# Causal mask carried by staircase rows in both score stacks, turn of the normalised rows placed between score units, keys of later batches written to DRAM in stack order

## The reference

```python
x = x + self_attn(layernorm(x), Wq, Wk, Wv, Wo)      # 16 heads of 8, rotary, causal
x = x + cross_attn(layernorm(x), ctx, W_kv, W_q, W_proj, b_proj)
x = x + moe(layernorm(x), gate_w, w1, b1, w2, b2)    # top 2 of 8, gelu, routed by the mean row
# inside self_attn:
attn = where(causal, -inf, q @ k.T / sqrt(8)); out = softmax(attn) @ v
```

## Time and profile before

| what | us |
|---|---|
| median of 3 runs | 183.94 (183.62 to 191.8) |
| the profiled execution | 183.63 |
| its span, first to last instruction | 181.8 |
| PE busy | 163.6 (90%) |
| DVE busy | 129.9 (71%) |
| ACT busy | 104.9 (58%) |
| POOL busy | 67.7 (37%) |

### The profile page before, as it was taken

How to read it: one execution, slowest core, us unless ns; L and a number is a source line. 1 busy time by engine, 2 the same in 40 slices (tenths; PEclk the granted TensorE clock), 3 DMA queues, 4 the chain that set the end, 5 groups by cost and what they waited for, 6 DMA issues and landing times.

```text
span 181.8 us, 4434 instructions
## 1 busy us (share of the span) xinstructions
PE 163.6 (90%) x1528; PEld 117.6 (65%) x1536; DVE 129.9 (71%) x500; ACT 104.9 (58%) x218; POOL 67.7 (37%) x132
## 2 busy tenths in 40 slices
PE   5778987979899799799999999999999998989994
PEld 4457765756666577467567556656666465879983
DVE  4488599597599879879988988999955463642110
ACT  2055531257566565665567766867746766972351
POOL 6836929178900660250232232201251071124220
PEclk9999998799999999999999999999999999999999
DMA  5914254157157245134035125104402501706400
GB/s 161 286 17 127 71 157 121 50 131 184 41 143 194 64 128 151 32 101 142 24 79 159 30 78 157 32 4 123 143 7 84 177 0 26 238 29 176 118 29 29
DMA packets 23329, 18.39 MB, mean 101 GB/s; under 512 B 2308, under 2 KB 21252, under 8 KB 22660
## 3 DMA queue, kind: packets, MB, share of 16 engines
q1 hardware_dynamic: 22552, 17.20, 34.0%
q10 hardware_dynamic: 756, 0.92, 1.8%
HBM read 12.08 MB, written 2.29 MB: 79 GB/s over the span
## 4 chain that ended last, share of the span: by engine, by line
PE 55%; DVE 23%; DMA 8%; issue 5%; SPq 3%; POOL 2%; ACT 2%; DVEq 0%; POOLq 0%; ACTq 0%
PE psV L975 11%; PE psA L929 9%; PE psB L953 8%; DVE negmax L663 8%; PE psA L1019 6%; DMA stackQ<-scratch 5%; PE psV L1036 4%; PE psM L843 4%; DMA ctx_tok<-ctx_dram 3%; DVE xn L616 3%; DVE masked L657 3%; PE psB L866 3%; PE psA L1036 2%; DVE stats L607 2%; PE psB L1019 2%
## 5 line engine op out<-in xcount | busy, mean ns | idle before, releaser
L797 ACT ACTIVATE E<-psB 128x512 f32<-128x512 f32 x112 | 62.1, 595 | 24.5 <-PE psB L958 10.2
L929 PE MATMUL psA<-stackK,stackQ 72*128 72x256 bf16 (+1 forms) x256 | 41.5, 260 | 5.1 <-DVE negmax L657 2.0
L663 DVE TENSOR_REDUCE negmax<-psA 128x2 f32<-128x512 f32 x64 | 40.6, 681 | 4.4 <-PE psA L929 4.2
L953 PE MATMUL psB<-stackQ,stackK 74*128 74x256 bf16 (+1 forms) x256 | 41.1, 259 | 0.4
L657 DVE CUSTOM_DVE_ANT_0 masked<-psA,row_mask 128x128 bf16<-128x128 f32 (+1 forms) x128 | 36.8, 347 | 6.0 <-PE psA L929 6.0
L929 PEld LDWEIGHTS psA<-stackK,stackQ 72*128 72x128 bf16 x256 | 21.7, 98 | 15.2 <-DVE negmax L663 3.0
L975 PE MATMUL psV<-E,V 128*18 128x256 f32 (+1 forms) x512 | 30.5, 356 | 0.0
L953 PEld LDWEIGHTS psB<-stackQ,stackK 74*128 74x128 bf16 x256 | 22.1, 97 | 6.7 <-ACT E L797 2.7
L513 POOL TENSOR_SCALAR rstd<-mv 128x2 f32<-128x2 f32 x12 | 2.7, 227 | 56.6 <-DVE mv L611 56.6
L975 PEld LDWEIGHTS psV<-E,V 128*18 128x18 f32 x512 | 11.9, 97 | 13.1 <-issue 6.6
L616 DVE TENSOR_SCALAR xn<-res,mv,rstd 128x128 f32<-128x128 f32 x24 | 10.0, 514 | 6.5 <-POOL rstd L514 6.4
(11 more groups left out here) (112 smaller groups left out, 249.5 us busy)
## 6 DMA issues: line engine op xcount, KB each, us to landing
stackK<-scratch SPq DMA_DIRECT2D x18, 192.0 KB
stackQ<-hid SPq DMA_DIRECT2D x36, 64.0 KB
w1s<-w_dram SPq DMA_DIRECT2D x8, 258.0 KB, 2.8
w2s<-w_dram SPq DMA_DIRECT2D x8, 256.0 KB, 4.2
stackQ<-scratch SPq DMA_DIRECT2D x2, 576.0 KB
stackK<-hid SPq DMA_DIRECT2D x16, 64.0 KB
scratch<-hid SPq DMA_DIRECT2D x4, 192.0 KB, 4.2
scratch<-parts_ctx SPq DMA_DIRECT2D x4, 192.0 KB, 6.6
```

Of the source, the lines that this page charges most:

```text
L663: dve.tensor_reduce(negmax[:, b, heads[0]:heads[-1] + 1:2, t], scores, AX_X, ALU.max, negate=True).then_inc(a_taken, 1)
L797: act.activation(dst, psB[:, bank].rearrange("p (h q) -> p h q", h=dst.shape[1]), ACT.Exp, scale=SCALE).then_inc(b_taken, 1)
L929: last = pe.matmul(psA[:, bank, i * keys:(i + 1) * keys], stackQ[0:ROWS, b, h, t * P:(t + 1) * P], stackK[0:ROWS, b, h, 0:keys], start=Tru ...
L953: last = pe.matmul(psB[:, bank, i * n:(i + 1) * n], stackK[:, b, h, t * P:(t + 1) * P], stackQ[:, b, h, q0:S], start=(s == 1 or i == 0), s ...
```

## The change

Four edits.

1. **Mask in the stacks.** The stacks get 48 more rows (`KEPT`; 120 in all, `CAUSAL`). Rows 72 to 119 hold a staircase of powers of two in keys (`kept_k`) and queries (`kept_q`) that makes the product over 120 rows of a diagonal 128x128 block hugely negative above the diagonal and leaves the rest alone. Rows 72, 73 are ones in `kept_k` and zeros in `kept_q`. POOL builds the two tiles (48 x 256) with 7 affine selects and 3 memsets in place of `mask16T` and `row_mask`. SP copies them, broadcast over 16 heads, to all batches (`stack_keep`): two DMAs of 768 KB for batches 0 and 1 together, two of 384 KB each for batch 2 and batch 3. A and B units of s=0 use 120 rows on the diagonal block and 72 or 74 elsewhere, so that products of 256 columns across a diagonal block become two of 128. The mask product L958 goes; job 0's A units, which run before the rows are there, get such a product instead. DVE takes maxima of s=0 with one reduction for a unit, as s=1 does. The two DMAs of ones go.
2. **`ln_turn`** of all jobs but the last moves from the end of one half to behind the first two units of the next.
3. **Keys in stack order.** `write_k` sends each part by its own DMA as soon as it is ready (3 of 64 KB instead of 1 of 192 KB) so that DRAM holds them in the order of the stack's rows; the source of each read is then [24 rows][8 KB].
4. New waits: PE's first A unit of a job and first B unit, and SP's first `max_rows`, wait for the kept rows (`kept_in`).

```diff
+KEPT = 48
+CAUSAL = ROWS + KEPT
-    start += [("stack_put", 0, 1), ("stack_fill", 0, 1)]
+    start += [("stack_put", 0, 1), ("stack_keep", 0, 0, 2), ("stack_fill", 0, 1), ("stack_keep", 0, 2, 1)]
+    put(14, "stack_keep", 0, 3, 1)
-        put(m + 4, "ln_turn", s + 1, b)
+        if (s, b) == (1, NB - 1):
+            put(m + 4, "ln_turn", s + 1, b)
+        else:
+            between.setdefault(m + 5, []).append(("ln_turn", s + 1, b))
-        order += [step for _, step in sorted(units, key=lambda unit: unit[0])]
+        units = [step for _, step in sorted(units, key=lambda unit: unit[0])]
+        order += units[:2] + between.get(half, []) + units[2:]
 # SP
+            def rows_k(s, b):
+                return scratch[s, b, 1].rearrange("i p t -> (i p t)").rearrange("(e t) -> e t", t=NH * S)
+            def write_k(s, b, src, ready):
+                rows = rows_k(s, b).rearrange("(d r) (h t) -> r d h t", r=NPART, h=NH)
+                for r in range(NPART):
+                    sp.wait_ge(ready, r + 1)
+                    sp.dma_start(rows[r], src[:, r]).then_inc((scr_k_self, scr_k)[s][b], 16)
             def read_k(s, b):
-                src = scratch[s, b, 1]
-                by_part = bass.AP(src.tensor, src.offset, [[NH * S, HD], [P * S, NPART], [1, NH * S]])
                 for i in range(NPART):
                     r = i * NPART * HD
-                    sp.dma_start(stackK[r:r + NPART * HD, b], by_part).then_inc(k_in[b], 16)
+                    sp.dma_start(stackK[r:r + NPART * HD, b], rows_k(s, b)).then_inc(k_in[b], 16)
-                sp.dma_start(stackK[MAXROW + i:MAXROW + i + 1].rearrange("o b h t -> o (b h) t"),
-                             half).then_inc(ones_in, 16)
+                if kind == "stack_keep":
+                    n = st["g"]
+                    for stack, kept in ((stackQ, kept_q), (stackK, kept_k)):
+                        sp.wait_ge(kept_set, len(KEY_STEPS) + len(QUERY_STEPS) + 1)
+                        src = kept[:, :, :].rearrange("r n q -> r (n q)").rearrange("r (o q) -> r o q", o=1)
+                        sp.dma_start(stack[ROWS:CAUSAL, b:b + n].rearrange("r b h q -> r (b h) q"),
+                                     src.to_broadcast([KEPT, n * NH, S])).then_inc(kept_in[b], 16)
                 if kind == "max_rows":
+                    if s == 0 and b == 0:
+                        sp.wait_ge(kept_in[0], 32)
 # DVE, scores_max
-                            last = dve.tensor_tensor_reduce(out=masked[...], in0=scores[:, i, 0:keys],
-                                                            in1=row_mask[:, S - keys:S], ..., accum_out=negmax[:, b, h, t:t + 1])
+                    dve.tensor_reduce(negmax[:, b, heads[0]:heads[-1] + 1:2, t], scores[:, :, 0:keys], AX_X, ALU.max, negate=True).then_inc(a_taken, 1)
 # PE, scores_max
+                        spans = [(k, P, CAUSAL if k == t * P else ROWS) for k in range(0, keys, P)]
+                    by_product = s == 0 and b == 0
+                    if by_product:
+                        last = pe.matmul(blocks, ident16[:, :], mask16[:, 0:len(heads), :], start=False, stop=True,
 # PE, scores_exp
+                        spans = [(q, P, CAUSAL if q == t * P else MAXROW + 2) for q in range(q0, S, P)]
-                    if s == 0:
-                        last = pe.matmul(blocks, ident16[:, :], mask16T[:, 0:len(heads), :], start=False, stop=True,
```

More of the change, by code:

```diff
@@ L51 @@
 MAXROW = ROWS
+KEPT = 48
+CAUSAL = ROWS + KEPT
+STEP = 3
 VW = 32
@@ L479, in then @@
                 pool.wait_ge(pool_own, own[0])
+            made = [0]
             def split(src, dst, ready):
@@ L506, in _, with stairs @@
             pool.memset(ident16[:, :], 0.0)
-            then(pool.memset(row_mask[:, :], 0.0))
             then(pool.memset(mask16[:, :, :], 0.0))
+            def stairs(rows, steps):
+                for least, below in steps:
+                    pool.affine_select(out=rows[:, :, :], in_=rows[:, :, :], compare_op=ALU.is_ge, fill=below,
+                                       base=2 * STEP - least, pattern=[[0, NT], [1, P]],
+                                       channel_multiplier=-STEP).then_inc(kept_set, 1)
+                    made[0] += 1
+                    pool.wait_ge(kept_set, made[0])
             def rsqrt_var(n, b):
@@ L649, in _ @@
                     scores = psA[:, bank].rearrange("p (h k) -> p h k", h=nh)
-                    if s == 0:
[L651 to L662, removed]
-                    dve.tensor_reduce(negmax[:, b, heads[0]:heads[-1] + 1:2, t], scores, AX_X, ALU.max, negate=True).then_inc(a_taken, 1)
+                    keys = (t + 1) * P if s == 0 else S
+                    dve.tensor_reduce(negmax[:, b, heads[0]:heads[-1] + 1:2, t], scores[:, :, 0:keys], AX_X, ALU.max, negate=True).then_inc(a_taken, 1)
                 if kind == "max_rows":
@@ L927, in _ @@
                     keys = (t + 1) * P if s == 0 else S
-                    for i, h in enumerate(heads):
-                        last = pe.matmul(psA[:, bank, i * keys:(i + 1) * keys], stackQ[0:ROWS, b, h, t * P:(t + 1) * P],
-                                         stackK[0:ROWS, b, h, 0:keys], start=True, stop=True)
+                    if s == 1 or b == 0:
+                        spans = [(0, keys, ROWS)]
+                    else:
+                        spans = [(k, P, CAUSAL if k == t * P else ROWS) for k in range(0, keys, P)]
+                    by_product = s == 0 and b == 0
+                    for i, h in enumerate(heads):
+                        for k, n, rows in spans:
+                            last = pe.matmul(psA[:, bank, i * keys + k:i * keys + k + n],
+                                             stackQ[0:rows, b, h, t * P:(t + 1) * P], stackK[0:rows, b, h, k:k + n],
+                                             start=(not by_product or i == 0), stop=not by_product,
+                                             skip_group_check=True)
+                    if by_product:
+                        blocks = psA[:, bank].rearrange("p (h k) -> p h k", h=len(heads))[:, :, t * P:(t + 1) * P]
+                        last = pe.matmul(blocks, ident16[:, :], mask16[:, 0:len(heads), :], start=False, stop=True,
+                                         skip_group_check=True)
                     last.then_inc(a_full, 1)
@@ L947, in _ @@
                     if unit == 0:
[L948 to L949 removed]
+                        pe.wait_ge(kept_in[0], 32)
                     if unit < 2:
                         pe.wait_ge(rope_first, NB)
+                    if s == 1:
+                        spans = [(0, S, MAXROW + 2)]
+                    else:
+                        spans = [(q, P, CAUSAL if q == t * P else MAXROW + 2) for q in range(q0, S, P)]
                     for i, h in enumerate(heads):
[L953 to L959 removed]
+                        for q, w, rows in spans:
+                            last = pe.matmul(psB[:, bank, i * n + q - q0:i * n + q - q0 + w],
+                                             stackK[0:rows, b, h, t * P:(t + 1) * P], stackQ[0:rows, b, h, q:q + w],
+                                             start=True, stop=True)
                     last.then_inc(b_full, 1)
```

64 lines of the change are left out of this document (29 added, 35 removed).

## The result

The changed kernel is slower: 189.96 us median of 6 runs (188.7 to 192.14) against 184.55 (183.62 to 191.8, 6 runs); the ratio is 1.027, with a 95% interval of 1.020 to 1.034. Its profiled execution took 188.7 us with a span of 186.9, 5.1 more than before. (Some executions of every kernel are disturbed by several per cent; the ratios leave them out.)

What follows compares the result with a forecast made beforehand. DVE and PE were taken to bound inside jobs, SP's DMA chain to gate the starts of jobs 2 to 4. Job starts summed to -1.0, -1.4, -1.5, -2.3, -2.9, then -3.5 at the end: 183.63 to 180.1 us, range 176.6 to 183.6.

Steps and rivals of the forecast that it cites:

- DVE maxima: Maxima of s=0 on DVE: 0.6 to 0.62 us each, gaining 1.5 us a job in jobs 0 to 3.
- PE: Mask products removed from B units, 7.0 us in all; 1.75 us added in job 0's A units; split products free.
- POOL: Selects and memsets building the mask tiles: 3.2 us (2.2 to 4.5) for selects, hidden in POOL's 4.11 us idle.
- Reads: Stack reads ahead of jobs 2 and 3: 12 DMA engines at 177 GB/s, 0.4 us gained (bounds 0 and 2.2).
- ln_turn: Moved turns: 0.3 us each in jobs 5, 6 and 7 where PE is on the path, nothing in jobs 2 to 4.
- Jobs 4 to the end: From the start of job 4 to the end of span: a further 2.0 us gained, from -1.5 to -3.5.
- The kept rows: SP's kept transfers from 17 us: 5.3, 2.7 and 2.7 us at 294 GB/s, the first done by about 23.
- The lower bound, 177 GB/s: Slow rate for the kept transfers, what the reads reach in 38.8 to 45.3: 8.9, 4.4 and 4.4 us.
- What hung on it: SP's issues behind the kept rows: batch 1's fills queue 0 to 2 us, second pair at about 29, max_rows at 33.8.
- rival D: Kept transfers crowd out batch 1's fills at 17 to 34 us: 95 GB/s, max_rows 8 us late, 188; chance 0.1.
- rival C: Kept rows slow at 177 GB/s: max_rows 3 us later, 183.1; milder by ports, about 218 GB/s, 181; chance 0.13.

Runs made afterwards that it cites:

- the run without rows: Changed kernel sending only two of the 48 kept rows, no product reading the others, causal mask left out but for job 0's first maxima: 181.82 us median.
- maxima alone: Kernel before with self-attention maxima taken over masked keys too, one reduction a unit, mask product kept: 182.37 against 184.02 us, ratio 0.993.
- with the other two parts: Kernel before with maxima over masked keys too, plus the change's ln_turn and keys in stack order, mask product kept: 180.2 us median, ratio 0.975.
- ln_turn alone: Kernel before with only ln_turn moved behind the first two units of the next half: 183.06 against 183.87 us, ratio 0.996.
- the mask alone: Changed kernel with ln_turn and the key path as before, only the mask in the stacks left: 191.7 to 197.9 us in four runs.
- their own runs: Kernel before with only ln_turn moved: ratio 0.996; kernel before with only keys in stack order: ratio 0.996.
- the seven transfers behind its end: Changed kernel with seven 768 KB transfers between various rows added behind its end, one at a time: 2.41 to 7.11 us each.
- the one edit that took 6 us of ACT's wait away: Changed kernel with ACT's read of batch 1's queries called for four halves later, the write staying: 189.88 us, ratio 1.032.
- the last run: Kernel before with maxima over masked keys, ln_turn and key order changed, mask rows for batches 2 and 3 sent at halves 18 and 26: 185.39 us median, ratio 0.997.

## Why the prediction was wrong, by its own steps

- **DVE maxima: right.** They are one reduction a unit, five in 3.08 us at 20.23, 0.62 each (forecast 0.6). DVE's busy time fell by 5.7 us, 1.4 a job (forecast 1.5).
- **PE: right in kind, too large in size.** The mask product is gone and products of 128 columns keep their pace: the first four of job 2 stand 0.24 us ahead of the next work (53.64 to 53.88), and so they do in the run without rows (45.79 to 46.03). The 12 mask products of job 0's A units lie before 32 us there (the last at 30.9); in the changed kernel the last is at 37.0. PE's sum was -5.25. Without the rows PE is busy 159.3 us against 163.6 before, but the kernel before ran 3.4 us at 1.2 GHz. Against the profiles with the old products and a clock of 1.00 (maxima alone 161.7, with the other two parts 163.5, ln_turn alone 163.9) the gain is 2.4 to 4.6. With the rows it is 2.1, as part of the work ran at 1.2 GHz (granted 0.50 from 30 to 34 us, after PE had been busy for 0.21 of the 4 us before).
- **POOL: right.** Busy +2.1 us, hidden: it ends its constants at 13.76 and next waits for DVE until 14.45. Its first split for batch 1 was ready for the fill at 20.08.
- **Reads: right.** From max_rows to the start of jobs 2 and 3 it is 11.25 and 11.24 us (forecast 11.4 and 11.5); the run without rows has 11.23 for job 2. The DMA share in between, 43.8 to 53.6, is 0.77 at 182 GB/s (forecast 0.7 at 177), with the last kept pair among it.
- **ln_turn: right in size**, -0.8 by its own run against -0.9, if one takes the middle of its interval.
- **Jobs 4 to the end: right**, -1.7 against -2.0.
- **The kept rows: the step that failed.** "294 at full share ... as packet size and SBUF source agree" gave 5.3 us for the first pair. It took 14.75 in company and would take 12 alone. The row chosen (ACT's write of 21 to 22) had the packet size of the kept rows but read all 128 partitions and wrote to DRAM; the kept rows read 48 partitions and write 48. The lower bound, 177 GB/s, was too high as well: measured were 107 in company, 130 alone. Beside it the sum had no term for the clock: 10.3 us ran at 1.2 GHz, against 3.4 before.
- **What hung on it: also wrong, in size.** "Batch 1's fills queue 0 to 2 us" became 6; the second pair did not go out "at about 29" but at 33.8; the writes of batch 2 were held for 6.56 us; max_rows was 8.0 us late where -0.6 was forecast.

This is rival D nearly line for line: "The kept transfers crowd out batch 1's fills", at 95 GB/s, 16.5 us, max_rows 8 us late, 188. Measured: 107 GB/s, 14.75 us, 8.0 us late, 188.7. I gave it a chance of 0.10 and left it out of the range. Its mechanism was the right one; its rate was luck. The row behind the 95 GB/s (24.2 to 25.2) holds 22 packets in all at a DMA share of 0.40, so it was low for want of work, whereas the kept rows moved slowly with the engines busy. Only rival C's sentence on ports spoke of few partitions, and I weighed it below a row that only had the same packets. D did not name ACT's wait, and did not have to: it hid behind the fills.

Not settled: how the 14.75 us divide between the slow rows and the transfers mixed among them; how much of the loss is the clock; and why the mask alone lies 2 to 4 us above the whole change when its missing parts are worth 0.8 each by their own runs. Its profile has 13.6 us at 1.2 GHz in place of 10.3, which may be a part of it. A second profile of the changed kernel, with the seven transfers behind its end, starts job 1 at 41.67 in place of 40.19, so that 1.5 us of it is within what repeats differ by.

## What to carry to other kernels

- Price a long transfer inside SBUF by the partitions at both ends, taken from a row with as few and as similar partitions, before its packet size or its bytes. It is not the count alone: 48 rows moved at 34% to 43% of the rate of 128 in most places and at 70% in rows 40 to 87. A tile read by such a transfer may be put in other rows than 0 to 47; no run tried that in the kernel.
- Constants broadcast by DMA compete with what is issued behind them, on the other queue too (ACT's write of 192 KB took 11.4 us, before 2.0), even where the issuing engine has a gap; compare the time that they fill the engines with the gap, and ask what is issued in it. And before moving a mask, ask whether the step needs it: the maxima did not.
- The engine with the longest wait in the profile need not be on the path: the one edit that took 6 us of ACT's wait away changed nothing, because the fills set the start. Look at the granted clock behind a wait of PE too: it fell in the changed kernel and in the last run, and did not in the run without rows.

## What the runs showed of the hardware that I had not expected

- 768 KB within SBUF took 2.41 us over 128 partitions, 3.46 from rows 40 to 87 to the same, 5.59 and 5.64 to rows 72 to 119 from there and from rows 64 to 111, and 6.0 to 7.1 out of rows 0 to 47, wherever they went. Large packets do not help.
- The DMA engines show as busy meanwhile, 0.9 at 175 GB/s in the changed kernel and in the first half of the transfer alone, where 128 partitions ran at 326 with a share of 1.08: a high share does not say how many bytes are moved.
- With the slow transfers ahead of it SP is held in the issue itself: three writes of 64 KB took 6.56 us to issue, against 1.89 in the run without the rows.
